# Squaring the rectified gram tile from SBUF in an image and graph kernel, with another split of the gathers

## The reference

```
# layer 0, per image: P = 2304 pixels, C = 64
nrm = maximum(sqrt(sum(xf * xf, axis=1)), EPS)
xn = xf / nrm
s = relu(einsum('bcp,bcq->bpq', xn, xn)) ** 2
g = einsum('oc,bcp->bop', Wc, xf) + bc
out = einsum('bpq,bcq->bcp', s, g)
# layer 1: graph attention over edge_index (2 x 262144) and self loops
h = x_flat @ W_gat
e = leaky_relu(a_src[src] + a_dst[dst]);  ee = exp(e - segment_max(e, dst)[dst])
alpha = ee / segment_sum(ee, dst)[dst]
agg = segment_sum(h[src] * alpha, dst)
scores = layernorm(agg).mean(heads);  two experts of four per pixel, softmax
out = sum over experts of gate * (gelu(x @ W1 + b1) @ W2 + b2)
```

## Time and profile before

| | us |
|---|---|
| median of 3 runs | 5282.03 |
| lowest and highest run | 5274.48, 5291.11 |
| profiled execution, whole | 5291.28 |
| its span, first to last instruction | 5289.5 |
| PE busy | 3533.1 (67%) |
| DVE busy | 3964.2 (75%) |
| ACT busy | 3392.4 (64%) |
| POOL busy | 2941.6 (56%) |

### The profile page before, as it was taken

The page is one execution under the profiler, slowest core; times in us unless marked ns, Lnnn a source line. Parts: engine busy times, 40 slices in busy tenths (PEclk is TensorE's granted clock), DMA queues, the critical chain, the costliest instruction groups (busy, mean ns, idle before and its releaser), DMA issues. The chain is left out here.

```text
span 5289.5 us, 70597 instructions
## 1 busy us (share of the span) xinstructions
PE 3533.1 (67%) x22687; PEld 1450.6 (27%) x22687; DVE 3964.2 (75%) x5512; ACT 3392.4 (64%) x4285; POOL 2941.6 (56%) x2937
## 2 busy tenths in 40 slices
PE   4888988500488888888898988884000017788778
PEld 1223333200243344343443444342000002222222
DVE  8998988997666666766666655555999848787877
ACT  4777988401676767776676776775566526566665
POOL 6000000048777777777777777777656147666661
PEclk9999999755699999999999999997555558888889
DMA  6100100002122222222222212224555527999997
GB/s 258 36 20 20 33 21 16 17 14 82 22 47 57 42 62 48 47 52 52 56 48 46 64 40 53 48 50 105 176 190 187 190 71 147 151 161 159 155 157 141
DMA packets 332482, 441.96 MB, mean 84 GB/s; under 512 B 183193, under 2 KB 261916, under 8 KB 331500
## 3 DMA queue, kind: packets, MB, share of 16 engines
q1 hardware_dynamic: 209744, 288.12, 19.8%
q0 software_dynamic: 105536, 148.61, 16.6%
q10 hardware_dynamic: 16896, 1.18, 0.2%
HBM read 252.35 MB, written 166.47 MB: 79 GB/s over the span
## 5 line engine op out<-in xcount | busy, mean ns | idle before, releaser
L980 POOL DMA_INDIRECT rows<-htab_d,idx x2048 | 2134.3, 1042 | 761.3 <-issue 603.9
L2406 DVE SCALAR_TENSOR_TENSOR s<-gram,rel 128x1024 f32<-128x1024 f32 (+1 forms) x720 | 798.1, 1116 | 800.1 <-ACT rel L2066 797.3
L2066 ACT ACTIVATE rel<-gram 128x1024 f32<-128x1024 f32 (+1 forms) x1080 | 1005.4, 940 | 540.5 <-PE gram L1876 533.1
L1830 PE MATMUL acc<-s,gT 128*64 128x512 f32 (+1 forms) x4320 | 1020.2, 552 | 0.0
L1876 PE MATMUL gram<-hl 128*64 128x512 f16 (+1 forms) x4320 | 787.9, 367 | 217.5 <-DVE s L2406 182.3
L1876 PE MATMUL gram<-hl,lh 128*64 128x512 f16 (+1 forms) x4320 | 775.5, 361 | 13.5 <-issue 13.5
L1761 POOL DMA_INDIRECT R<-seg_d,nidx x576 | 587.7, 1020 | 191.3 <-issue 165.9
L1930 PE MATMUL ye<-hid,w 128*64 128x384 f32 x1536 | 376.2, 570 | 260.5 <-DVE ms L2625 195.8
L1080 POOL IOTA slots<- 64x2048 int32 x1 | 1.8, 1833 | 975.5 <-POOLq L192 975.5
L2158 ACT ACTIVATE hid<-up,b1t 128x768 f32<-128x768 f32 x384 | 333.8, 900 | 261.4 <-PE up L1942 260.1
L1876 PEld LDWEIGHTS gram<-hl 128*64 128x64 f16 x4320 | 244.5, 110 | 708.2 <-DVE s L2406 467.3
(11 more groups left out here) (372 smaller groups left out, 5401.4 us busy)
## 6 DMA issues: line engine op xcount, KB each, us to landing
gs<-gates_d SPq DMA_DIRECT2D x64, 1024.0 KB
rows<-htab_d,idx POOLq DMA_INDIRECT x2048
seg_d<-state SPq DMA_DIRECT2D x32, 996.0 KB, 8.9
raw_d<-w_zeros POOLq DMA_DIRECT2D x48, 512.0 KB, 23.2
raw_d<-rows POOLq DMA_DIRECT2D x32, 768.0 KB
tne<-tn_d SPq DMA_DIRECT2D x32, 576.0 KB
x2e<-x_d SPq DMA_DIRECT2D x32, 576.0 KB
out<-res SPq DMA_DIRECT2D x64, 256.0 KB
```

Of the source, the lines that this page charges most:

```text
L980: pool.indirect_dma_start(out=n.rows[:, k % 2, j, :], out_offset=None, in_=n.htabx, in_offset=bass.IndirectOffsetOnAxis(ap=n.idx[:, g % 2, ...
L1830: last = pe.matmul(acc[(par + c) % 2][j * C:(j + 1) * C, 0:w], gT[:, par, 2 * k + j, :], s2[:, u % SLOTS, j * w:(j + 1) * w], start=k == 0 ...
L2066: act.activation(rel[:, t % RELS, 0:2 * w].rearrange("p (j x) -> p j x", j=2), gram[(par + t) % 2][:, :, 0:w], ACT.Relu, scale=1.0 / SPLIT ...
L2406: dve.scalar_tensor_tensor(halves(s2[:, t % SLOTS, 0:2 * w]), gram[(par + t) % 2][:, :, 0:w], 1.0 / SPLIT ** 2, halves(rel[:, t % RELS, 0: ...
```

## The change

DVE squares `rel`, with both inputs in SBUF and the same tile, in place of multiplying gram (PSUM) with rel. Since DVE reads gram no longer, PE waits in every step for ACT's `rel` of step t - 2 alone. `AHEAD` goes from 29 to 26 chunks (1856 to 1664 gathers ahead of the first segment), `PIECE` from 8 to 13.

```diff
@@ -1278,8 +1278,8 @@
-    AHEAD = 29
-    PIECE = 8
+    AHEAD = 26
+    PIECE = 13
@@ -1864,10 +1864,7 @@
                     o, w = CH[c]
-                    if t % 3 == 2:
-                        pe.wait_ge(a_rel, STEPS * own + (t - 1))
-                    else:
-                        at_least(pe, v_s2, by_dve(STEPS) * own + by_dve(t - 1))
+                    at_least(pe, a_rel, STEPS * own + (t - 1))
                     bank = gram[(par + t) % 2]
@@ -2402,9 +2399,7 @@
                     if t % 3:
                         dve.wait_ge(a_rel, STEPS * own + t + 1)
-                        halves = lambda ap: ap.rearrange("p (j x) -> p j x", j=2)
-                        dve.scalar_tensor_tensor(halves(s2[:, t % SLOTS, 0:2 * w]), gram[(par + t) % 2][:, :, 0:w], 1.0 / SPLIT ** 2,
-                                                 halves(rel[:, t % RELS, 0:2 * w]), ALU.mult, ALU.mult).then_inc(v_s2, 1)
+                        dve.tensor_tensor(s2[:, t % SLOTS, 0:2 * w], rel[:, t % RELS, 0:2 * w], rel[:, t % RELS, 0:2 * w], ALU.mult).then_inc(v_s2, 1)
```

## The result

The changed kernel takes **5408.48 us** (5395.78 to 5418.53), the kernel before in the same comparison 5282.9 us: ratio **1.0237**, 95% interval 1.0209 to 1.0264. It is slower, as forecast, but by 126 us and not by 271. The profiled execution has a span of 5409.9 us against 5289.5, so 120 us are to be explained from the trace.

A forecast was written before the change was run, and what follows sets the result against it. POOL's gather issue was taken to bound the kernel from 1408.8 to about 4111 us. A later first segment load (+33) and the split (+238) gave +271 us, hence 5553 us; own range 5470 to 5640, 8-in-10 range 5365 to 5680.

The forecast's parts named there:

- Part 1: Image stage: PE waits for rel, not s, saving 6.0 us per image; stage 2223 to 2079 us, hidden under POOL.
- rival 3: Image stage stays at 2223 us because PE then waits for ACT's rel; 5562 us, chance 0.06.
- Part 2: DVE's square from SBUF takes 1.225 us against 1.223 for the operation removed: no gain or loss on DVE.
- Part 3: Image stage: squares with two SBUF inputs hold POOL's gathers, 0.224 us each on average, rate 1.331 to 1.555 us.
- the first term: Start of the segment stage: POOL's end sets the first segment load, 3692 in place of 3658.6, +33 us.
- Part 4: Segment stage: 192 more gathers left there, 13 a visit; visits 18.5 to 24.8 us, +238 us, bounds 207 and 262.
- The premise: POOL heads the path from 1408.8 to about 4111 us, so a faster image stage gives nothing by itself.
- Rival 1: Image stage: squares don't hold the gathers, rate stays 1.331 us, images' end sets the first load; 5373 us, chance 0.12.
- Rival 2: Image stage: gathers and squares lock, 3 gathers in 5.2 us, 1.74 us each; 5732 us, chance 0.12.
- Rival 4: Segment stage: DVE, not POOL, paces the visits, so 13 gathers fit in; faster, 5223 us, chance 0.04.

The follow-up runs named there:

- one_input_split: The changed kernel with an operation reading rel once from SBUF in place of the square (squaring left out in two of three steps): 5410.42 us, ratio 1.0247.
- square_alone: The changed kernel with the old split (AHEAD 29, PIECE 8), keeping the SBUF square and PE's wait for rel: 5436.59 us, ratio 1.0281.
- square_old_wait: The kernel before with the square from SBUF only: PE still waits for s, split 29 / 8: 5455.25 us, ratio 1.0310.
- after_old_wait: The changed kernel (split 26 / 13) with PE waiting for DVE's s as before: 5482.43 us, ratio 1.0383.
- ahead27: The changed kernel with AHEAD = 27 in place of 26, PIECE still 13: 5401.33 us, ratio 1.0221.
- The padding: Four waits on a reached semaphore before each of the first 1664 gathers: 5481.72 us on the kernel before with split 26 / 13, 5417.71 us on the changed kernel.
- in_flight6_before: The kernel before with six gathers in flight in place of four: 5282.58 us, ratio 1.0004.
- one_input: The changed kernel with split 29 / 8 and, in place of the square, an operation reading rel once (squaring left out in two of three steps): 5268.47 us, ratio 0.998.

## Why the prediction was right or wrong

**Part 1, the image stage: right in kind, half in size.** PE's wait for s went, and an image takes 2145.6/24 = 89.4 us in place of 92.6, that is 3.2 us less and not 6.0; the stage ended at 3554 and not at 3488. The waits of PE's matmul queue in 1800 us (1600 to 3400, some 20 images) show what took its place:

```profile
PE gram L1873 <- ACT rel L2063: 58.1, 31, 2.8
PE gram L1873 <- issue: 46.1, 16, 6.4
PE misc L1816 <- DVE hx L2394: 18.5, 20, 1.0
...
PE acc L1830 <- DVE s L2402: 11.2, 20, 0.6
```

Of these, "issue" was 40.7 us and hx 7.2 us before. So 58.1 + 5.4 + 11.3 + 11.2 = 86 us are new, 4.3 us an image, and 7.6 - 4.3 = 3.3. The next latest was ACT's rel, with 58.1 us. The prediction let four fifths of the stall go without asking whose turn it then was; rival 3 named ACT, and it was half right. PE's own work per image stayed: 81.1 us busy before, 81.4 after. The granted clock over the stretch fell from 0.99 to 0.96, still at the upper level of 2.4 GHz for nearly all of it; one_input_split has the same 0.96, so it doesn't come from the held gathers.

**Part 2, the square: right.** 1228 ns forecast as 1.225 us. The 1.127 us that the prediction worked out from the Trainium skill (VectorE: DVE Perf Modes, the TRN2 errata) wasn't there. The same section's formula for an fp32 `tensor_tensor` add, (N + 151)/0.96 ns, gives by estimate 1.224 us for 1024, and 1.228 agrees with it.

**Part 3, the hold: the right mechanism, and the term that was mis-sized. This is the step that failed.** Forecast 0.224 us a gather, measured 0.10 (1093 - 993 ns), 0.085 by start to start (1.421 against 1.337 us between 1600 and 3400), since landing waits shrink; square_alone, square_old_wait, after_old_wait and ahead27 show 0.09 to 0.11. Two errors:

- The wait was taken as the rest of the square. A gather ends 0.82 us after the square, but a free one takes 0.95 us anyway, so it loses 0.13 us less than that rest, and one begun in the first 0.045 us loses nothing. The prediction's own row had it: 1.35 us for a gather begun 0.54 us before the end of tk is a wait of 0.40 and not of 0.54. (Under the S scan the prediction's times give 0.75 us after the end, 3765.73 less 3764.98, and not the 0.81 that it names.) With 24 x 0.56 + 6 x 0.135 us^2 over 89.4 us (the wait integrated over the starts that are held) the mean is 0.159 us by this estimate, 0.149 of it under the wide squares.
- The starts are not even. 310 of 1267 lie 0.1 to 1.1 us into a wide square (even spacing would give 24 x 1.0/89.4 = 27%, 340), with a mean wait of 0.43 us where even spacing gives 0.50; 133 of them begin 0.8 to 1.0 us into the square, where little is left to wait. That brings the wide squares from 0.149 to 0.113 us (the table's 0.106 and 0.007 for the nine held ones begun before 0.1 us). Why the starts gather there, I can only argue: a held gather is followed by others at fixed 1.25 us, and the squares come at PE's own fixed pace. The padding that should have tested it did not act.

Then the sum took POOL's end for the start of the segment stage. POOL was at 3531, the images' end set the first `got`, and this term came out at -86 us in place of +33. The formula was right that the later of the two decides; with 1.418 us it changed sides. For the first `got` the border lies at (3572.7 - 1408.8)/1498 = 1.444 us a gather, and for the first scan at about 1.452, since the marks of the first segment land later still (a `got` at 3584 would have done). Rates of 1.42 to 1.455 were measured, so the changed kernel sits close to it.

The errors can be told apart by putting them into the prediction's own sum one by one. With 1.331 + 0.085 = 1.416 us a gather and all else as forecast, POOL ends at 3526 and the first term is -133 in place of +33: 166 us of the miss are the size of the hold. The images' end at 3554 in place of 3488 gives back 47 us (3572.7 less 3526), and part 4 takes 32: 271 - 166 + 47 - 32 = 120. So the error of part 1 partly cancels the other two by luck; without it the forecast would have missed by 198 us and not by 151.

**Part 4, the split: right sign, 16% too large, and one claim wrong.** +206 us between the first and the 25th `got` against +238, just below even the lower bound of 207. The missing 32 us are nearly all in the 19 visits up to index 19: 441 us and not 19 x 24.8 = 471, 23.2 us each (median 23.0). One of them in the changed kernel (POOL, then DVE's G and S):

```profile
3781.81 0.94 POOL L1716 DMA_INDIRECT got<-raw_d,edge  x1 [0.30 <-issue]
3783.05 1.59 POOL L1718 DMA_INDIRECT nb<-htab_d,node  x1 [0.30 <-issue]
3784.95 3.28 POOL L980 DMA_INDIRECT rows<-htab_d,idx  x1 [0.30 <-issue]
3788.54 0.95 POOL L980 DMA_INDIRECT rows<-htab_d,idx  x1 [0.31 <-issue]
...
3804.20 2.19 POOL L1716 DMA_INDIRECT got<-raw_d,edge  x1 [0.30 <-issue]
```

```profile
3782.30 1.53 DVE L2497 TENSOR_TENSOR G<-GT,G 128x1312 f32<-128x1312 f32 x1 [0.55 <-ACT G L2113]
3783.87 3.62 DVE L2500 TENSOR_TENSOR_SCAN S<-G 128x1660 f32<-128x1660 f32 x1
```

At the longer period POOL's visit meets G and S with its first issues: G holds `nb`, S holds the first gather to 3788.23. The big loads land at 3787.46 and 3790.09, ahead of the fifth gather behind them (3792.29), the first that has to wait for a landing. No wait for a landing is left in the visit; from 3600 to 4000 POOL waited 10.7 us for landings, and before, from 3700 to 4080, 81.6 us. "The five added gathers of a visit can't move into the 4.10 us wait" was wrong: that wait ran from the issue of the loads, and anything that delays POOL behind them uses it up. What was forecast as the only possible saving (the scan's 1.67 us falling into the wait) happened the other way round: the wait fell into the scan. For this visit, 22.39 us against the 18.48 of the earlier trace rows, the step of 3.91 is 5 x 1.25 for the gathers, less 4.10, + 0.66 (S holds for 2.33 us in place of 1.67) + 0.64 (G on `nb`) + 0.46 for smaller holds; the median visit is 23.0 us.

The hole ahead of segment 20 was there, and deeper, 98 us and not 70:

```profile
4141.08 3.37 DVE L2479 COPY_PREDICATED AE<-moveg,AE 128x72 f32<-128x72 uint8 x7 [97.79 <-ACT AE L2107]
```

From the 25th `got` on nothing changed, as forecast (164.6 and 1013.9 us).

**The premise.** "POOL runs at the head of the path from 1408.8 to about 4111" was right for the changed operands with 29 chunks ahead (square_alone). For the kernel before it was closer than the prediction had it, twice: the first scan waited for the images' side, with POOL 2.5 us ahead of it, and in the visits DVE set the pace and POOL just kept up (in_flight6_before). "A faster image stage gives nothing by itself" is thus off by 2.5 to 5 us. The whole answer is two maxima in a row: POOL or the images' end, then POOL or DVE. The three parts don't add up because of them: +149 us (square and wait alone) and +203 us (split alone) give +126 together.

**The rivals.** 5408 lies in the wide range (5365 to 5680), but outside the forecast's own (5470 to 5640). Rival 1 (squares don't hold gathers, 5373) came nearest in time, for a wrong reason: its consequence, POOL ready before the images' end, came true through a smaller hold. Rival 2 (1.74 us) fell at 1.42. Rival 4's premise, that DVE paces the visits, was right for the kernel before; its price fell at a visit of 23 us, which fifteen issues and the holds of G and S fill.

None of these kernels beats the one before in a form that still squares; one_input shows that an operation with a single SBUF input would be worth 0.1 to 0.3%, if there were one that squares.

## What to carry to other kernels

When a stage ends at the later of two engines, write down both ends and the rate at which they change places before summing: here 1.444 us a gather, against a forecast of 1.555 and a measured 1.42. If one engine is held by another's instructions, take the wait as (end of the holder + tail) less the time it would have taken anyway, from a row that shows a partial wait. Moving an input from PSUM to SBUF is no neutral edit where GpSimd issues indirect DMAs: count the DVE operations with two SBUF inputs, and look in the trace for others that hold, as the `tensor_scalar` on bytes here. And follow what the next stage's first instruction really waits for: here it was a small load that SP had put behind the experts' tables.

## What the runs showed of the hardware

- A gather begun 0.05 to 1.1 us into a DVE operation of 1.23 us with two SBUF inputs ends 0.818 us after it, whatever its start. DVE isn't slowed: 1228 ns against 1218 with one input and 1223 with PSUM, and the 303 squares begun while a gather was being issued took 1225 ns on average.
- An operation of the same shape on DVE takes 1.22 to 1.23 us with one SBUF input, with two, and with one in PSUM and one in SBUF.
- A `tensor_scalar` on 328 bytes a partition, with one SBUF input, holds a gather as well (17 of 17 in the kernel before).
- Four waits on a reached semaphore ahead of each gather don't show in the usual gap on POOL: it stays 0.305 us.
- SP's load of `moveg`, for which the first scan waits, took 7.3 us from issue to landing in the changed kernel, 12.4 in the kernel before and 14.5 in in_flight6_before. What made it longer no run here separates.
